# Two-layer latent model on one Trainium2 core: VectorE, ScalarE and GpSimd work of the rotary cross-attention put in another order, and the value weights prepared by three engines

## The reference

```python
x = x + _L0_xattn_ref(_layernorm(x), ctx_1024, cos, sin, ..., Wq, Wkv, Wo, bo)   # this stage
x = x + _L0_attn_ref(...); x = x + _L0_ffn_ref(...)
x = x + _L1_xattn_ref(...); x = x + _L1_attn_ref(...); x = x + _L1_ffn_ref(...)

# inside _L0_xattn_ref
lat = layer_norm(latents, ln_lat_g, ln_lat_b)
ctx = layer_norm(context, ln_ctx_g, ln_ctx_b)
q = (lat @ Wq)                                  # 16 heads of 64
k, v = split(ctx @ Wkv)
k = apply_rope(k, cos, sin)                     # x1*cos - x2*sin, x2*cos + x1*sin
attn = clip(einsum('bhnd,bhsd->bhns', q, k) * scale, -11, 11)
out = einsum('bhns,bhsd->bhnd', softmax(attn), v)
return out @ Wo + bo
```

## Time and profile before

| | us |
|---|---|
| three runs | 1217.03, 1219.90, 1221.51 |
| median | 1219.9 |
| profiled execution, device time | 1220.99 |
| its span in the trace | 1219.2 |

### The profile page before, as it was taken

One profiled execution on the slowest core, in us unless ns is written; L12 is line 12 of the kernel. 1 busy time (PEld: TensorE's weight loads), 2 busy tenths in 40 slices (PEclk: granted clock), 3 DMA queues, 4 the chain that ended last, 5 costly groups with the idle time before them and its releaser, 6 DMA issues.

```text
span 1219.2 us, 23526 instructions
## 1 busy us (share of the span) xinstructions
PE 1162.7 (95%) x9792; PEld 948.5 (78%) x9792; DVE 810.3 (66%) x1383; ACT 566.8 (46%) x922; POOL 230.9 (19%) x178
## 2 busy tenths in 40 slices
PE   7699999999999999999899999999999999999998
PEld 5587878878787878774546667888889999999997
DVE  3958677777697685756778886356665665665663
ACT  4425252425343434322539998374544544445451
POOL 2025261716253535341100000010000000000000
PEclk9799999999999999999989999999999999999999
DMA  7103030302030302074142324300544554454440
GB/s 291 35 20 102 20 103 18 105 11 94 19 105 18 105 18 69 29 286 196 48 173 105 140 105 174 138 3 6 237 173 174 206 198 162 190 206 177 169 171 18
DMA packets 32192, 140.73 MB, mean 115 GB/s; under 512 B 3163, under 2 KB 3419, under 8 KB 21604
## 3 DMA queue, kind: packets, MB, share of 16 engines
q1 hardware_dynamic: 32100, 139.42, 30.7%
HBM read 138.88 MB, written 0.52 MB: 114 GB/s over the span
## 4 chain that ended last, share of the span: by engine, by line
PE 46%; DVE 3%; issue 2%; ACT 2%; DMA 0%; DVEq 0%; ACTq 0%
PE mid_bk L57 10%; PE mid_bk L58 10%; PE mid_bk L59 10%; PE mid_bk L1198 5%; PE mid_bk L1213 2%; PE mid_bk L1243 2%; PE mid_bk L1169 2%; PE mid_bk L1088 2%; PE mid_bk L1233 1%; DMA w_raw<-in_w 0%; PE mid_bk L1342 0%; DVE mo_w_lo L1875 0%; DVE mo_w_lo L1881 0%; ACT sa_sc L1508 0%; PE mid_bk L1294 0%
## 5 line engine op out<-in xcount | busy, mean ns | idle before, releaser
L631 POOL TENSOR_TENSOR norm_both<-norm_both,prob 128x512 f32<-128x512 f32 x118 | 159.1, 1348 | 208.5 <-DVE prob L407 201.1
L59 PE MATMUL mid_bk<-mo_x_hi,mo_w_lo 128*128 128x256 f32 x496 | 140.4, 283 | 0.0
L58 PE MATMUL mid_bk<-mo_x_lo,mo_w_hi 128*128 128x256 f32 x496 | 140.4, 283 | 0.0
L57 PE MATMUL mid_bk<-mo_x_hi,mo_w_hi 128*128 128x256 f32 x496 | 140.3, 283 | 0.0
L557 ACT ACTIVATE prob<-u_ps 128x512 f32<-128x512 f32 x128 | 66.2, 605 | 135.7 <-PE u_ps L757 135.6
L1881 DVE TENSOR_TENSOR mo_w_lo<-w_raw,mo_w_hi 128x2048 fp32r<-128x2048 f32 x32 | 73.3, 2291 | 74.5 <-ACT mo_w_hi L1590 74.5
L57 PE MATMUL k_ps<-ctx_hi,wk_hi 128*128 128x512 f32 x256 | 103.4, 404 | 13.8 <-issue 7.5
L1590 ACT ACTIVATE mo_w_hi<-w_raw 128x2048 fp32r<-128x2048 f32 x32 | 61.2, 1913 | 91.1 <-PE mid_bk L59 91.1
L58 PE MATMUL k_ps<-ctx_lo,wk_hi 128*128 128x512 f32 x256 | 101.2, 395 | 0.0
L59 PE MATMUL k_ps<-ctx_hi,wk_lo 128*128 128x512 f32 x256 | 101.0, 394 | 0.0
L57 PE MATMUL mid_bk<-mo_w_hi,mo_h_hi 128*128 128x512 f32 x256 | 101.0, 394 | 0.0
(11 more groups left out here) (278 smaller groups left out, 2515.6 us busy)
## 6 DMA issues: line engine op xcount, KB each, us to landing
w_raw<-in_w SPq DMA_DIRECT2D x64, 1024.0 KB, 6.3
wk_raw<-in_wk_rows SPq DMA_DIRECT2D x32, 512.0 KB, 3.3
ctx_raw<-in_ctx_rows SPq DMA_DIRECT2D x8, 1024.0 KB, 5.5
x_k<-in_ctx_T SPq DMA_DIRECT2D x8, 1024.0 KB, 6.9
x_val<-in_ctx_heads SPq DMA_DIRECT2D x8, 1024.0 KB, 4.9
tabs<-in_rot_tabs SPq DMA_DIRECT2D x8, 512.0 KB, 3.3
vals<-in_wq_rows SPq DMA_DIRECT2D x4, 512.0 KB, 7.6
wv_raw<-in_wv_rows SPq DMA_DIRECT2D x4, 512.0 KB, 12.1
```

What stands on the lines that cost most here:

```text
L57: pe.matmul(out, w_hi, x_hi, start=start, stop=False)
L58: pe.matmul(out, w_hi, x_lo, start=False, stop=False)
L59: return pe.matmul(out, w_lo, x_hi, start=False, stop=stop)
L631: ins = pool.tensor_tensor(to, to, src, ALU.add)
```

## The change

Nothing is computed differently; the output is made by the same operations. What moves:

- **GpSimd, chunk boundary.** In the step r = 3 the splits of the next chunk come first. The probability sums of two steps, `add_up(t-2)` and `add_up(t-1)`, follow them. Before, `add_up(t-2)` had run in the step r = 2, ahead of the splits.
- **VectorE, chunk boundary.** `sums(n)` moves from behind `turn_second(4n)` to the head of the step r = 0, ahead of `low_k` and `turn_first`. `low_s(n)` moves from the step r = 1 into r = 0, behind `clip`. `stats` of a chunk moves from r = 0 to r = 3 of the chunk before that, ahead of `clip`; `spread` stays in r = 0.
- **ScalarE.** `high_s(n)` moves ahead of `exponent(4n-1)`. `root(n+1)` moves from the step r = 0 to the head of r = 2.
- **Start.** `weight_sums` moves from VectorE to GpSimd, and two of the seven low parts with it (`low_weights`). ScalarE makes `high_k(0)` and three of `high_v` between the queries. TensorE's wait for all low parts is split up by product. The semaphore `idle_set` becomes `prepared`, and counts these too.

```diff
@@ -174,7 +174,7 @@
...
                  "summed", "weighed", "o_out", "den_mm", "den_out", "recip", "normalised", "y", "added", "bo_in",
-                 "bo_added", "rounded", "idle_set")
+                 "bo_added", "rounded", "prepared")
         s = {n: sem("x0_" + n) for n in names}
@@ -220,7 +220,8 @@
...
                 "S2": (1, 0, 0), "S4": (1, 1, 0), "S3": (1, 0, 1), "S1": (1, 1, 1)}
-        w_of = {"B11": 0, "B21": 1, "B22": 2, "T3": 3, "T1": 4, "T2": 5, "T4": 6}
+        w_of = {"B11": 0, "T1": 1, "T2": 2, "T3": 3, "T4": 4, "B21": 5, "B22": 6}
+        NWD = 5
         full = {n: ctx_full[:, 2 * kh:2 * kh + 2, 256 * th:256 * th + 256]
@@ -266,8 +267,8 @@
...
             load_tab(0)
-            for i, to in ((0, 0), (2, 3), (3, 2), (1, 1)):
-                load_wv(i, to)
+            for i, to in ((0, "B11"), (2, "T3"), (3, "B22"), (1, "B21")):
+                load_wv(i, w_of[to])
             load_ctx(1)
@@ -319,17 +320,9 @@
...
         def _(dve):
-            def weight_sums():
-                dve.wait_ge(s["wv_in"], 64)
-                for n, (dst, a, b) in enumerate((("T1", "T3", "B11"), ("T2", "B22", "T1"), ("T3", "B22", "T3"),
-                                                 ("T4", "B21", "T2"))):
-                    dst, a, b = (wv_raw[:, w_of[m], :, :] for m in (dst, a, b))
-                    if n:
-                        dve.wait_ge(s["part_sum"], n)
-                    dve.tensor_tensor(dst, a, b, ALU.subtract).then_inc(s["part_sum"], 1)
-
             def low_v(j):
-                dve.wait_ge(s["part_hi"], j + 1)
+                dve.wait_ge(s["part_hi"], j + 3 if j else 1)
+                dve.wait_ge(s["prepared"], (2, 3, 5, 5, 5)[j])
                 dve.tensor_tensor(wv_lo[:, j, :, :], wv_raw[:, j, :, :], wv_hi[:, j, :, :],
@@ -345,7 +338,7 @@
...
                     if m:
-                        dve.wait_ge(s["part_sum"], 4 + 4 * n + m)
+                        dve.wait_ge(s["part_sum"], 4 * n + m)
                     dve.tensor_tensor(full[dst], full[a], full[b], op).then_inc(s["part_sum"], 1)
@@ -429,35 +422,35 @@
...
             low_k(0)
-            weight_sums()
-            for j in range(3):
-                low_v(j)
             for t in range(NT + 1):
                 n, r = t // 4, t % 4
-                if t < NT and r == 2 and n + 1 < NC:
-                    center(dve, n + 1)
-                if t + 1 < NT:
-                    low_k(t + 1)
                 if t < NT:
-                    if r == 1:
-                        low_s(n)
+                    if r == 0:
+                        sums(n)
+                    if r == 2 and n + 1 < NC:
+                        center(dve, n + 1)
+                    if t + 1 < NT:
+                        low_k(t + 1)
                     turn_first(t)
...
                     turn_second(t)
-                    if t == 0:
-                        for j in range(3, NWB):
-                            low_v(j)
-                    if r == 0:
-                        sums(n)
+                    if r == 3 and n + 2 < NC:
+                        stats(dve, n + 2)
                 if t >= 1:
...
                 if t < NT:
+                    if t == 0:
+                        for j in range(NWD):
+                            low_v(j)
+                    if r == 0:
+                        low_s(n)
+                        if t == 0:
+                            stats(dve, 1)
+                        if n + 1 < NC:
+                            spread(dve, n + 1)
                     if r == 1:
                         add_products(n, 0)
-                    if r == 0 and n + 1 < NC:
-                        stats(dve, n + 1)
-                        spread(dve, n + 1)
                 if t == 11:
@@ -500,10 +493,11 @@
...
         def _(act):
-            def high_v(j):
+            def high_v(w):
                 act.wait_ge(s["wv_in"], 64)
-                if j >= 3:
-                    act.wait_ge(s["part_sum"], 4)
+                if w in ("T1", "T2", "T3", "T4"):
+                    act.wait_ge(s["prepared"], 1 + int(w[1]) if w != "T3" else 4)
+                j = w_of[w]
                 act.activation(wv_hi[:, j, :, :], wv_raw[:, j, :, :], ACT.Copy).then_inc(s["part_hi"], 1)
@@ -513,7 +507,7 @@
...
             def high_s(n):
-                act.wait_ge(s["part_sum"], 4 + 4 * n + 4)
+                act.wait_ge(s["part_sum"], 4 * n + 4)
                 for u in range(2):
@@ -568,21 +562,26 @@
...
             queries(1)
+            high_k(0)
             queries(2)
+            high_v("B11")
+            high_v("B21")
+            high_v("B22")
             queries(3)
-            high_k(0)
-            for j in range(3):
-                high_v(j)
             for t in range(NT + 1):
...
                         context(n + 1, k, k)
+                if t < NT and r == 2 and n + 1 < NC:
+                    root(act, n + 1)
                 if t + 1 < NT:
...
                 if t == 0:
-                    for j in range(3, NWB):
-                        high_v(j)
+                    for w in ("T1", "T2", "T3", "T4"):
+                        high_v(w)
+                if t < NT and r == 0:
+                    high_s(n)
                 if t == 18:
@@ -597,10 +596,6 @@
...
                     exponent(t - 1)
-                if t < NT and r == 0:
-                    high_s(n)
-                    if n + 1 < NC:
-                        root(act, n + 1)
                 if t < NT and r == 1:
@@ -633,15 +628,35 @@
...
 
-            pool.memset(part[:], 0.0).then_inc(s["idle_set"], 1)
+            def weight_sums():
+                pool.wait_ge(s["wv_in"], 64)
+                for m, (dst, a, b) in enumerate((("T1", "T3", "B11"), ("T2", "B22", "T1"), ("T3", "B22", "T3"),
+                                                 ("T4", "B21", "T2"))):
+                    dst, a, b = (wv_raw[:, w_of[w], :, :] for w in (dst, a, b))
+                    pool.wait_ge(s["prepared"], m + 1)
+                    pool.tensor_tensor(dst, a, b, ALU.subtract).then_inc(s["prepared"], 1)
+
+            def low_weights():
+                pool.wait_ge(s["prepared"], 5)
+                for m, w in enumerate(("B21", "B22")):
+                    pool.wait_ge(s["part_hi"], m + 2)
+                    j = w_of[w]
+                    pool.tensor_tensor(wv_lo[:, j, :, :], wv_raw[:, j, :, :], wv_hi[:, j, :, :],
+                                       ALU.subtract).then_inc(s["prepared"], 1)
+
+            pool.memset(part[:], 0.0).then_inc(s["prepared"], 1)
             for k in range(KD):
                 split(0, k)
+            weight_sums()
+            low_weights()
             for t in range(NT + 1):
-                n = t // 4
-                if t < NT and t % 4 == 3 and n + 1 < NC:
+                n, r = t // 4, t % 4
+                ahead = t < NT and n + 1 < NC
+                if ahead and r == 3:
                     for k in range(KD):
                         split(n + 1, k)
-                if t >= 1:
+                    add_up(t - 2)
+                if t >= 1 and not (ahead and r == 2):
                     add_up(t - 1)
@@ -699,20 +714,21 @@
...
                 v = 2 * n + ip
-                if n == 0 and ip == 0:
-                    pe.wait_ge(s["part_lo"], NWB)
                 if ip == 1:
...
                         pe.wait_ge(s["exped"], 16 * n + bank + 1)
+                    if n == 0 and ip == 0:
+                        pe.wait_ge(s["part_lo"], (1, 3, 4, 4)[bank])
                     if bank == 1:
-                        pe.wait_ge(s["part_lo"], NWB + 2 * n + 2)
+                        pe.wait_ge(s["part_lo"], NWD + 2 * n + 2)
                     if v == 9 and bank >= 2:
...
                 pe.wait_ge(s["v_kept"], 2 * v + 1)
+                pe.wait_ge(s["prepared"], 7)
                 product(n, ip, "A12", "B21", 0, False, True)
@@ -805,7 +821,7 @@
...
 
-            pe.wait_ge(s["idle_set"], 1)
+            pe.wait_ge(s["prepared"], 1)
             for _ in range(3):
```

## The result

The changed kernel takes 1242.4 us (median of 4 runs, 1239.35 to 1246.6), the kernel before 1218.47 beside it (1215.4 to 1221.51): ratio 1.0199, 95% interval 1.0158 to 1.024. It is slower by about 2%. The profiled execution took 1246.6 us, the longest of the four, with a span of 1244.8, 25.6 more than the earlier trace rows.

What follows compares the result with a forecast made beforehand. TensorE is busy nearly throughout, so only its waits count. The profiled 1220.99 us plus 28.9 for the boundaries and 1.0 for the start gives 1250.9, less 1.1 at the median's level: 1250 us, 8-in-10 range 1222 to 1258.

Steps and rivals of the forecast that it cites:

- What the change takes away: TensorE's waits at the seven chunk boundaries, for the exponent, issue, product sums and `low_s`: 21.2 us, all taken as gone.
- The new wait before `project(4n+1, 0)`: At chunk boundaries TensorE waits for VectorE's `turn_first(4n)`: 6.5 us in chunks 2, 4, 6; 41.5 over seven.
- a turn: At boundaries a VectorE operation with both inputs in SBUF waits for one whole GpSimd operation: 1.15 us, four times.
- the 6 to 7 that I had named as a sign: In the profile after, the four context sums (L349) would take 6 to 7 us instead of 2.86.
- The first rival: At boundaries VectorE keeps the ports through a run, as against GpSimd's copy: about −14 us there, 1200 in all; 14%.
- The copy: GpSimd's first operation in chunks 1 and 5: staying out costs 2.5 and 3.7 us, getting in 6.5 and 7.7; middle taken.
- The clock: After new TensorE waits of 4 us or more the clock falls: 1.9 us lost each, 11.4 over the boundaries.
- The sum: Seven boundaries: new waits 41.5 plus clock loss 11.4, minus 21.2 and 2.8 of waits that go, net +28.9 us.
- the last term of the 24.0: Another 0.4 us of waiting gone at each boundary, between 425.88 and 444.96: 2.8 for seven.
- The start: Up to the first sixth product, VectorE's operations take turns with GpSimd's moved weight work: +1.0 us.
- the chain of twelve operations: At the start, six GpSimd and six VectorE operations all in a row take 20.2 us, ending at 43.0.
- the 40 below which I had said that I am wrong: Sign at the start: the forecast is wrong if TensorE starts `project(1, 0)` before 40.

Runs made afterwards that it cites:

- held-back: The changed kernel with GpSimd's probability sums of step r = 2 waiting until VectorE made the next chunk's first turned pair: 1219.71 us, ratio 0.9997.
- narrow sum: The changed kernel with the probability sums of r = 2, chunks 0 to 6, done on one column of each 128: 1204.2 us, ratio 0.9874.

## Why the prediction was right, point by point

- **What the change takes away.** Right: the 21.2 us of the earlier trace rows at the boundaries are gone.
- **The new wait before `project(4n+1, 0)`.** Right in place, cause and size: forecast 41.5 us for the seven boundaries, measured 38.6. The held-back and the narrow sum show the cause: without GpSimd at that moment, the same order on VectorE waits 1.8 us on average. The terms: I priced a turn at 1.15; the four sums took 5.71, below the 6 to 7 that I had named as a sign, 0.95 more than alone for each of the three that wait, and `low_k` 1.1 more, together 3.9 instead of 4.6. That is 0.7 of the 1.2 by which 6.5 became 5.3. The other 0.5 lies ahead of the turns: VectorE began the statistics 7.6 us before TensorE was ready (436.79, against 449.75 − 5.32 = 444.43), where I had 7.1.
- **Who is next when both queue.** The first rival (VectorE keeps its place through a run) falls; L342 in 5.71 us is the row. The copy, whose case I left in the middle, gets in too between the sums, which wait for each other: four of them take 5.04 and 5.03, and chunks 1 and 5 wait 5.37 and 6.56, against 4.5 and 5.7. Between two operations that do not wait for each other it did not get in, as in the row at 355.48; the kernel after, GpSimd and VectorE ahead of the sums of chunk 5:

```profile
373.79 1.28 DVE L468 TENSOR_TENSOR attn_T<-attn_T,q_T 128x512 f32<-128x512 f32 x2
373.93 2.21 POOL L628 COPY norm_both<-prob 128x512 f32<-128x512 f32 x1 [4.33 <-DVE prob L400]
```

Whether the semaphore or the kind of operation decides, no run separates. Chunk 3 waits 1.2 more than chunk 2 for its two additions (L464 in the kernel before), where I had 1.3.
- **The clock.** The 24 products of `project(4n+1, 0)` and `project(4n+1, 1)` behind each stall took 7.3 to 8.5 us where they take 5.7 undisturbed; that is 15.4 us in seven, 2.2 each, where I had 1.9 for five and half of it for two, 11.4. The sum of stalls and clock is 54.0 against 52.9.
- **The sum.** The stage ends 26.7 us later (589.00 against 562.27), 2.0 less at the start, so 28.7 for the boundaries; forecast 28.9. Part of this is luck, errors that cancel: 2.9 too much for the stalls, 4.0 too little for the clock. 38.6 + 15.4 − 24.0 is 30.0, which leaves 1.3. Most of that is a slip in the last term of the 24.0: I took 2.2 us between 425.88 and 444.96 as shown waiting, and the earlier trace rows show 1.45 + 0.52 = 1.97, so that the 2.8 for seven boundaries should have been some 4.
- **The time itself.** 1250 forecast, 1242.4 measured, 7.6 less, inside the range. Of this 3.0 is the start and 0.2 the boundaries. Another 1.2 is the part behind `project(30, 0)`, which I took as unchanged. The last 3.1 lies between executions: the profiled one of the kernel after is 4.2 above its median, that of the kernel before 1.1. So 28.7 is what the boundaries cost in the longest execution; the others have a granted clock of 0.974 to 0.976 against its 0.971, and whether their boundaries cost as much is not shown.
- **The start.** Forecast +1.0, measured −2.0. The step that failed is the length of the chain of twelve operations: it ended at 40.2 and not at 43.0. A 128x1024 of GpSimd and a sum of VectorE took 2.8 us together (11.22 for four); I had added 2.55 and 0.65 in full. The alternation itself was there. `project(1, 0)` started at 41.61, past the 40 below which I had said that I am wrong. `add_products` then came at 60.8 and not 63.6.
- **The root.** I took the wait for `exponent(4n)` as gone with the root's move, and that alone made a faster kernel (1213.05), though in its trace only 2.6 us of that lie in the stage. I also took the waits of 1.4 before `project(4n, 0)` as a gain of GpSimd's new order. The waits did go, but they are not what this order is worth, and the sum did not show it: alone it costs 10 us (1228.74), as it puts a probability sum beside the clip and the turning. In the changed kernel that delay of VectorE is part of the larger wait; how much of it was not measured.

The Trainium skill ("SBUF — State Buffer", section "Who interferes with whom") lists the tensor-scalar operations with those that can take both ports, and a two-input operation from SBUF as one that collides with GpSimd's reads. The clip and L306 in the run with GpSimd's order alone (2.52 for 1.42, 1.25 for 0.17) agree with the first, and the stretched sums, `low_k` and `low_s` above with the second. I had put the clip among those that go free.
